# Counting the edges of each node: the node number split at 6 bits instead of 7, batches of 22 columns instead of 8, and the destinations requested one stage earlier

## The reference, cut to what matters

```
src = concatenate([s, d, loop]);  dst = concatenate([d, s, loop])
order = argsort(dst);  src, dst = src[order], dst[order]
agg = segment_sum(message(src, edge attributes), dst, num_segments=3750)
```

## Time and profile before

| | us |
|---|---|
| time, median of 3 runs | 9475.49 (9473.54 to 9476.48) |
| the profiled execution, its own time | 9459.24 |
| its span | 9457.5 |
| POOL busy | 6656.1 |
| PE busy | 7101.5 |
| DVE busy | 5926.1 |
| ACT busy | 3121.1 |

### The profile page before, as it was taken

The page is one execution under the profiler, slowest core; times in us unless marked ns, Lnnn a source line. Parts: engine busy times, 40 slices in busy tenths (PEclk is TensorE's granted clock), DMA queues, the critical chain, the costliest instruction groups (busy, mean ns, idle before and its releaser), DMA issues. The chain is left out here.

```text
span 9457.5 us, 158810 instructions
## 1 busy us (share of the span) xinstructions
PE 7101.5 (75%) x35186; PEld 5063.2 (54%) x35186; DVE 5926.1 (63%) x21108; ACT 3121.1 (33%) x10505; POOL 6656.1 (70%) x7024
## 2 busy tenths in 40 slices
PE   6555546666686666669999957777677777799999
PEld 4222224343343333334444446666566666799999
DVE  7666645444434444446665567777677777799888
ACT  2222210000020000000000045555455555699998
POOL 3777777777725777767777767777577777477776
PEclk9999999999995555555555567777777777899999
DMA  4222223111153111111111122222122222211111
GB/s 111 89 88 87 85 78 99 53 53 53 53 217 105 53 53 53 53 54 52 53 53 53 50 60 60 60 60 60 51 60 60 60 60 60 84 53 53 52 52 51
DMA packets 292477, 636.18 MB, mean 67 GB/s; under 512 B 124830, under 2 KB 160801, under 8 KB 279585
## 3 DMA queue, kind: packets, MB, share of 16 engines
q0 software_dynamic: 223872, 420.21, 16.8%
q1 hardware_dynamic: 68032, 210.12, 6.5%
HBM read 478.99 MB, written 150.87 MB: 67 GB/s over the span
## 5 line engine op out<-in xcount | busy, mean ns | idle before, releaser
L1058 POOL DMA_INDIRECT relsum_rows<-relation_table,tab_idx x1994 | 1891.0, 948 | 836.8 <-issue 496.1
L1101 PE MATMUL relsum_sums<-relsum_hot,relsum_rows 128*128 128x128 f32 x3988 | 1556.5, 498 | 930.8 <-DMA relsum_rows<-relation_table,tab_idx 689.0
L1101 PEld LDWEIGHTS relsum_sums<-relsum_hot,relsum_rows 128*128 128x128 f32 x3988 | 994.4, 312 | 1490.0 <-DMA relsum_rows<-relation_table,tab_idx 1477.6
L1001 POOL DMA_INDIRECT conv_rows<-tensor_table,src_idx x997 | 943.6, 946 | 404.2 <-issue 213.6
L1058 POOL DMA_INDIRECT gcnsum_rows<-x_table,src_idx x997 | 952.5, 955 | 333.5 <-issue 178.2
L1001 POOL DMA_INDIRECT gat2sum_rows<-gat_table,src_idx x997 | 944.4, 947 | 303.8 <-issue 235.5
L1001 POOL DMA_INDIRECT gat1sum_rows<-gat_table,src_idx x997 | 943.7, 947 | 303.8 <-issue 222.7
L668 POOL DMA_INDIRECT records<-sort_recs,place_rows x968 | 927.1, 958 | 295.1 <-issue 295.1
L1068 DVE TENSOR_SCALAR relsum_hot<-iota_row,dst_rel,w 128x128 f32<-128x128 f32 x1994 | 708.9, 356 | 429.1 <-issue 419.7
L1101 PE MATMUL gcnsum_sums<-gcnsum_hot,gcnsum_rows 128*128 128x128 f32 x1994 | 781.6, 495 | 0.0
L2095 ACT ACTIVATE conv_rows_attr<-conv_rows,conv_rec 128x64 f32<-128x64 f32 x2991 | 754.9, 334 | 50.5 <-SPq L2054 43.7
(11 more groups left out here) (392 smaller groups left out, 15104.0 us busy)
## 6 DMA issues: line engine op xcount, KB each, us to landing
relation_table<-table_row SPq DMA_DIRECT2D x30, 2048.0 KB, 6.3
relation_table<-sort_space SPq DMA_DIRECT2D x40, 1024.0 KB
relsum_rows<-relation_table,tab_idx POOLq DMA_INDIRECT x1994, 2.5
place_lo_wide<-lo_rows SPq DMA_DIRECT2D x121, 256.0 KB, 3.4
relation_table<-place_extra SPq DMA_DIRECT2D x20, 1024.0 KB
gcnsum_rows<-x_table,src_idx POOLq DMA_INDIRECT x997, 2.5
gat1sum_rows<-gat_table,src_idx POOLq DMA_INDIRECT x997, 2.5
gat2sum_rows<-gat_table,src_idx POOLq DMA_INDIRECT x997, 2.5
```

Of the source, the lines that this page charges most:

```text
L1001: pool.indirect_dma_start(bufs[:, t % depth, :], None, table, bass.IndirectOffsetOnAxis(ap=idx[:, t:t + 1], axis=0)).then_inc(landed[t % l ...
L1058: pool.indirect_dma_start(rows[:, t % depth, :], None, table, bass.IndirectOffsetOnAxis(ap=idx[:, t:t + 1], axis=0)).then_inc(landed[t % d ...
L1101: pe.matmul(bank[:, 0:P], rows[:, t % depth, :], hot[:, t % HOTS, :], start=True, stop=True).then_inc(s["multiplied"], 1)
```

## The change

The destination number is split at 6 bits: `low` (0 to 63) and `top` (0 to 59). The one-hots are `hot_low` (64 rows) and `hot_top` (60 rows), each over `CB` = 22 columns, so that there are 44 batches and the entries of one column lie 22 numbers of 2 bytes apart. The matmul of a column now has 64 weights and 60 moving columns. The mix of chunk c comes after batch 2c + 3. The split into 7 bits and the rest, which placing still needs, is still made, but its casts move from DVE to ACT, and the eight transposes of `lo` move from ahead of the loop to after its batch 1. The counts come out with node numbers interleaved by two, so the first positions take four small matmuls in place of two, with a second triangular matrix that POOL makes. The destinations are loaded by SP in setup, ahead of x, into a tile that setup allocates; DVE clears its tail there.

```diff
+CB = 22
@@ setup, vector
+            dve.memset(dst[96:P, TAIL:], N).then_inc(zeroed.sem, 1)
             dve.memset(env.x[:, BLKS - 1:, :], 0.0).then_inc(zeroed.sem, 1)
@@ setup, sync
+            sp.wait_ge(zeroed.sem, 1)
+            load_lanes(sp, dst, inp["dst"], dst_in.sem)
             sp.dma_start(env.x[:, 0:BLKS - 1, :], ...
-            sp.wait_ge(zeroed.sem, 1)
+            sp.wait_ge(zeroed.sem, 2)
@@ count_edges
+    half_p, tops = P // 2, 2 * BLKS
+    batches = EC // CB
-        hot_lo = sb("hot_lo", [P, bufs, P, SB], F16)
-        hot_hi = sb("hot_hi", [P, bufs, BLKS, SB], F16)
-        iota_wide = sb("iota_wide", [P, P, SB], F16)
+        hot_low = sb("hot_low", [P, bufs, half_p, CB], F16)
+        hot_top = sb("hot_top", [P, bufs, tops, CB], F16)
+        iota_wide = sb("iota_wide", [P, half_p, CB], F16)
@@ vector
+            dve.tensor_scalar(low_i, dst[:, :], half_p - 1, None, ALU.bitwise_and)
+            dve.tensor_scalar(top_i, dst[:, :], 6, None, ALU.arith_shift_right)
...
-            for b in range(SBATCHES):
+            for b in range(batches):
...
-                dve.tensor_tensor(hot_hi[:, b % bufs, :, :], over_rows(hi[:, now], BLKS), iota_wide[:, 0:BLKS, :], ALU.is_equal)
-                dve.tensor_tensor(hot_lo[:, b % bufs, :, :], over_rows(lo[:, now], P), iota_wide[:, :, :],
+                dve.tensor_tensor(hot_top[:, b % bufs, :, :], over_rows(top[:, now], tops), iota_wide[:, 0:tops, :], ALU.is_equal)
+                dve.tensor_tensor(hot_low[:, b % bufs, :, :], over_rows(low[:, now], half_p), iota_wide[:, :, :],
@@ tensor
-            for b in range(SBATCHES):
+            for b in range(batches):
                 pe.wait_ge(s["hot"], b + 1)
-                for k in range(SB):
-                    mm = pe.matmul(cnt[:, 0:BLKS], hot_lo[:, b % bufs, :, k], hot_hi[:, b % bufs, :, k], ...
+                for k in range(CB):
+                    mm = pe.matmul(cnt[0:half_p, 0:tops], hot_low[:, b % bufs, :, k], hot_top[:, b % bufs, :, k], ...
                 mm.then_inc(s["counted"], 1)
-                if b % 3 == 1 and 0 < b // 3 <= chunks:
-                    mix(b // 3 - 1)
+                if b % 2 == 1 and 0 < b // 2 <= chunks:
+                    mix(b // 2 - 1)
+                if b == 1:
+                    pe.wait_ge(s["prepared"], 1)
+                    ... the eight transposes of lo
+            for i, weights in enumerate((env.above[0:half_p, :], above_odd[:, :])):
+                pe.matmul(sums[:, 0:BLKS], weights, count1[:, i, :], start=i == 0, stop=i == 1)
+            for i in range(2):
+                mm = pe.matmul(sums[:, BLKS:2 * BLKS], env.ones[0:half_p, :], count1[:, i, :], start=False, stop=True, ...
@@ scalar
+            act.copy(ident[:, :], env.ident[:, :])
+            act.wait_ge(s["split"], 1)
+            act.copy(lo[:, :], lo_i)
+            act.copy(hi[:, :], hi_i).then_inc(s["prepared"], 1)
```

More of the change, by code:

```diff
@@ L126, in over_rows, with setup @@
     return ap.unsqueeze(1).to_broadcast([ap.shape[0], count, ap.shape[1]])
-def setup(env, inp):
+def setup(env, inp, till_sorted):
     nc = env.nc
@@ L223, in slot_rows, with load_lanes, sort_edges @@
     return dve.scalar_tensor_tensor(rows_out, low, float(TILES), tile_no, ALU.mult, ALU.add)
-def sort_edges(env, inp, records, relation_layers, weights_dram, table):
+def load_lanes(sp, to, frm, done):
+    whole = frm[0:(P - 1) * EC].rearrange("(p c) -> p c", c=EC)
+    sp.dma_start(to[0:120, :], whole[0:120, :]).then_inc(done, 16)
+    sp.dma_start(to[120:P - 1, :], whole[120:P - 1, :]).then_inc(done, 16)
+    sp.dma_start(to[P - 1:P, 0:TAIL], frm[(P - 1) * EC:E].rearrange("(p c) -> p c", p=1)).then_inc(done, 16)
+def sort_edges(env, inp, dst, records, relation_layers, weights_dram, table):
     nc = env.nc
@@ L284, in count_edges @@
         mixed = sb("mixed", [P, 2, 2 * cols], F32)
+        low_i, top_i = (mixed[:, k, 0:EC].bitcast(I32) for k in range(2))
         basis = space[0:mixers * BASES, :]
@@ L391, in _ @@
+            dve.tensor_scalar(count1[:, :, :], cnt[0:half_p, 0:tops].rearrange("p (b i) -> p i b", i=2), 1.0, None,
+                              ALU.add).then_inc(s["count1_ready"], 1)
             dve.wait_ge(s["summed"], 1)
@@ L413, in mix @@
                           stop=True).then_inc(s["mixed"], 1)
[L415 to L418, removed]
-            for b in range(SBATCHES):
+            for b in range(batches):
                 pe.wait_ge(s["hot"], b + 1)
-                for k in range(SB):
-                    mm = pe.matmul(cnt[:, 0:BLKS], hot_lo[:, b % bufs, :, k], hot_hi[:, b % bufs, :, k], start=b + k == 0,
-                                   stop=b == SBATCHES - 1 and k == SB - 1)
+                for k in range(CB):
+                    mm = pe.matmul(cnt[0:half_p, 0:tops], hot_low[:, b % bufs, :, k], hot_top[:, b % bufs, :, k], start=b + k == 0,
+                                   stop=b == batches - 1 and k == CB - 1)
@@ L424, in _ @@
                 mm.then_inc(s["counted"], 1)
-                if b % 3 == 1 and 0 < b // 3 <= chunks:
-                    mix(b // 3 - 1)
-            pe.wait_ge(s["count1_ready"], 1)
-            pe.matmul(sums[:, 0:BLKS], env.above[:, :], count1[:, :], start=True, stop=True)
-            pe.matmul(sums[:, BLKS:2 * BLKS], env.ones[:, :], count1[:, :], start=True, stop=True).then_inc(s["summed"], 1)
+                if b % 2 == 1 and 0 < b // 2 <= chunks:
+                    mix(b // 2 - 1)
+                if b == 1:
+                    pe.wait_ge(s["prepared"], 1)
+                    for j in range(SB):
+                        mm = pe.transpose(turn_ps[0:SBATCHES, j * P:(j + 1) * P], lo[:, j * SBATCHES:(j + 1) * SBATCHES], ident[:, :])
+                    mm.then_inc(s["lo_turned"], 1)
@@ new lines, in _ @@
+            pe.wait_ge(s["above_made"], 2)
+            pe.wait_ge(s["count1_ready"], 1)
+            for i, weights in enumerate((env.above[0:half_p, :], above_odd[:, :])):
+                pe.matmul(sums[:, 0:BLKS], weights, count1[:, i, :], start=i == 0, stop=i == 1)
+            for i in range(2):
+                mm = pe.matmul(sums[:, BLKS:2 * BLKS], env.ones[0:half_p, :], count1[:, i, :], start=False, stop=True,
+                               skip_group_check=True)
+            mm.then_inc(s["summed"], 1)
```

78 lines of the change are left out of this document (41 added, 37 removed).

## The result

The changed kernel takes 9536.55 us (median of 4 runs, 9534.06 to 9539.56), beside 9475.12 us of the kernel before (4 runs, 9473.54 to 9476.48): a ratio of 1.0065, 95% interval 1.0050 to 1.0079, or 61.4 us slower. The prediction said 9534, in a range of 9486 to 9547. The profiled execution took 9534.06 us, its span is 9532.3.

What follows compares the result with a forecast made beforehand. The prediction took the barrier before placing as the bound, set by the chain over PE's mixes: 58.7 + 0.5 - 1.0 = +58 us on 9475.5 gives 9534, range 9486 to 9547.

Steps and rivals of the forecast that it cites:

- The place and the path: Barrier before placing: POOL alone bounds placing, so the barrier moves all; the mix chain, 1.0 us to spare before, ends last.
- The term of the column: PE's counting matmuls: 60 moving entries at 2.03 ns make 122 ns a column, against 61 before; bounds 27 and 128 ns.
- Rival (a): Counting columns on PE: spacing costs nothing, weight load binds, about 60 ns a column; +17 us, 9493; chance 0.20.
- (b): Counting columns on PE: one side pays part, 75 to 110 ns; 28 to 51 us later, 9503 to 9526; chance 0.12.
- (c): PE in counting reaches its faster clock level, columns under 36 ns, mix 1.0 us: 9468; chance 0.10 together with (d).
- 6 ns for handing over: Counting column on PE: added to the weight load's 53 ns at the transposes' rate, giving about 60 ns.
- the 6 us of the same name in the range: Upper end of the range: another 6 us for handing over, on top of 7 more, giving 9547.
- The cycle: Mix cycle on PE in counting: 5.37 + 0.15 + 2.0 = 7.52 us against 3.61; 15 cycles make 58.7 us later.
- The start: Setup to first mix: barrier 1 to 3 us later, loop starts at 16 to 18, first mix +0.5, basis load covers.
- DVE: DVE's one-hot tiles in counting: 1.54 us a batch, 29 us less in all, hidden behind PE in the mix cycles.
- The end: End of counting: loop about 180 us; ACT's last mix copy 149.0, then 57.5 us to SP's arrival at 206.5.
- The sum of +58: Barrier before placing: 58.7 from the cycles + 0.5 for the first mix - 1.0 slack = +58 us.

Runs made afterwards that it cites:

- e6: Changed kernel with three of four attribute loads and copies moved from behind the last mix to between the mixes: 9490.18 us against 9456.00 for the kernel before, ratio 1.0036.
- e10: Kernel before with three of four attribute loads and copies moved between the mixes: placing starts at 148.72 us, 0.54 us earlier.
- e3: Changed kernel with only the moving one-hot stored column by column, so 60 moving entries packed, 64 weights 44 bytes apart: column 124.8 ns against 125.5.
- e1: Changed kernel with 64 zero weight columns added, so each column matmul loads 128 weights, and two buffers for three: column 108 ns.
- e5: Changed kernel with the split back at 7 bits (128 weights, 30 moving), 22-column batches kept, two buffers: 9475.46 us against 9456.00 for the kernel before, ratio 1.0021.
- e4: Changed kernel with both one-hots stored column by column, so weights and moving entries packed: column 52 ns, DVE batch 2.98 us, cycle 5.96 us.
- e8: Changed kernel in batches of 4 columns instead of 22, entries 8 bytes apart, still 44 columns between mixes: column 59 ns behind a mix, cycle 6.18 us, placing at 187.07.
- e7: Changed kernel with 7-bit split, 22-column batches, early destinations, attributes between mixes, a mix after each batch from 7: 9440.79 us against 9456.00 for the kernel before, ratio 0.9986.
- e9: Kernel before with only the destinations requested early, in setup ahead of x: 1.0 us more, placing at 150.15 us.

## Why the prediction came out

**The place and the path were right.** Everything was said to hang on the barrier before placing, with the chain over the mix ending last: the difference at POOL's first placing record is 60.8 us of 61.4; e6 and e10 show the chain: the same edit takes 26 us off the start of placing in the changed kernel and 0.5 in the kernel before.

**The term of the column was right as a size and came from the wrong operand.** The prediction had 60 moving entries x 2.03 = 122 ns, and 128 as the bound from the weights. Measured: 125.5, and it is the weights (e3 leaves it at 124.8). The moving entries cost 1.76 each, not 2.03. At that price 30 of them take 53 ns, less than the 61 of before, so the 61 were most likely the weights'. This is an estimate: 1.76 was measured with 60 entries 44 bytes apart, not with 30 at 16 bytes, and no run took the 61 apart. That the number hit is luck: 64 x 1.95 and 60 x 2.03 lie 3 ns apart. With another split the same step would have missed: for 128 weights and 60 moving entries it gives 122, and e1 measured 108.

The Trainium skill's page "TensorE: Matmul & The Clock Gate", section "Weight-path perf modes", reads a full load of 128 weights in four chunks of 32 columns, packed or strided. The Trainium skill's page "SBUF — State Buffer", section Door 1, wants two hits in each line of 16 bytes. The runs agree with both: 128 spaced weights cost 65.6 ns or less in e5, which is 32 steps of 2.05, and 64 spaced weights 125.5, which is 64 steps of 1.96; at 8 bytes, two entries a line, 59 ns, near the packed 52. The prediction cited the two rules one by one, and let the first stand only against the packed rate of the transposes. Taken together they fit what was measured; that the full load runs in four chunks no run here shows, and 64 and 128 are the only numbers of weights that were run in the loop.

**Rival (a)**, 60 ns a column because the spacing costs nothing in this kind of load, was given 0.20 and is refuted: a column of 52 exists in e4, only with both operands packed. (b) and (c) are too: the column is over their 110, and the mix's record is as long as before, so PE stayed at the slower level. Rival (a)'s 6 ns for handing over, and the 6 us of the same name in the range, stand in no row; the forecast does not use them. The durations of the mix in after:

```profile
L433 PE MATMUL count_mix<-sort_space,count_coeff_t x32: 1056/1135/1217, 32.3 to 149.1; 32*128 32x512 f32 x32
```

**The cycle** came out at 7.72 against 7.52. 44 x 3.5 ns = 0.15 is the column, 0.05 what lies between. Over 15 cycles, with 3.61 for before in both, that is 61.7 instead of 58.7.

**The start.** First mix at -0.7 instead of +0.5 us, within what was given for the basis load. Setup's barrier came 1.7 us later (8.8 against 7.1), within the 1 to 3. The loop starts at 16.91, within 16 to 18, although the first integer step took 2.83 us and not 0.58 (below). The basis load covers this, as was said: PE still waits 1.12 us for it.

**DVE** was 1.54 us a batch, as predicted, and hidden, with 80.2 us of waiting.

**The end.** The loop's work on the counts ends at 182.4, forecast about 180, hidden. ACT's last copy of the mix ends 1.8 us later than forecast (150.8 against 149.0), and from there to SP's arrival it is about 58.1 instead of 57.5. In sum placing starts at 210.1 instead of 207. The sum of +58 is 2.6 short: the cycles lack 15 x 0.20 = 3.0, the chain behind the mixes 0.6 and SP's slack 0.2, and the first mix gives back 1.2.

**What the prediction did not tell** is that a large part of its own sum was the spacing of the mixes and not the split. That DVE's saving was worthless was clear. But its cycle holds 20 columns more than before's, and they are 15 x 20 x 61 ns = 18 us at the old column and 15 x 20 x 122 ns = 37 of its 58.7 us at the new one. Mixes placed closer would have bought back what the loop's own end (182.4) allows, some 26 us by the estimate under e5.

## What to carry to other kernels

In these runs a column's step was the larger of two prices, that of the weights and that of the moving entries, each by how its own entries lie in memory. Estimate both by themselves, from rows where the other one can't decide, before you scale a measured step with either. Before you make tiles longer to spare an engine, look for what is paced by the loop and comes due only once in so many iterations, and count how many columns the ring still holds (e8); here it was the mix, and its chain ended at the barrier with 1.0 us to spare. Where two chains end within a microsecond of each other, a gain needs both shortened (e7), and one edit alone shows nothing (e9, e10) or only its loss (e5).

## What the runs showed of the hardware

- In counting, whose float32 mix records last 1135 ns against 592 in a later stage (both at a granted clock that reads 1.00), which is TensorE's slower level, a load of 64 float16 weights 44 bytes apart costs 125 ns (e3) and one of 128 such weights 65.6 or less (e5). Half of the weights cost at least 1.9 times as much.
- With both operands' entries 8 bytes apart a column is nearly as cheap as packed: 59 ns against 52 (e8, e4). At 44 bytes before's form of column costs 65.6 ns and at 16 bytes 61.
- A DVE tile of 1408 float16 elements takes 884 ns if the repeated operand is read row by row, and 1615 if each of its elements is repeated innermost (e4). The Trainium skill's page "Vector Engine (DVE) Microarchitecture Reference", section 5.1, "Performance modes", says that one element read 16 times by an operation with two sources and 2-byte operands ran at the single rate on trn2. The rows agree: 1615 ns is 1.8 times 884.
- DVE's first integer step after setup took over four times as long as the third, which has the same form. DVE's timeline of after:

```profile
9.88 2.83 DVE L389 TENSOR_SCALAR count_mixed<-dst 128x968 int32<-128x968 int32 x1
12.63 0.92 DVE L390 TENSOR_SCALAR count_mixed<-dst 128x968 int32<-128x968 int32 x1
13.47 0.65 DVE L391 TENSOR_SCALAR count_attrs<-dst 128x968 int32<-128x968 int32 x1
```

A memset of POOL's (L490, 9.34 to 11.45 us) and the issue of the loads lie beside it. In the kernel before the same memset lies at 7.09 to 9.20 us, and DVE's cast of only 128 elements to `ident`, which begins at 8.24 beside it, took 1.54 us. So the memset is the first suspect; no run tried it.
